# Rates of the recurrence loaded straight into their masked places, tokens issued by GpSimd

## The reference, cut to what matters

```python
delta = xs @ W_delta
Bv = xs @ W_B
Cv = xs @ W_C
deltaA = jnp.exp(jnp.einsum('bld,dn->bldn', delta, A))
deltaB = jnp.einsum('bld,bln->bldn', delta, Bv)
def step(state, inp):
    dA_i, dB_i, x_i, C_i = inp
    state = dA_i * state + dB_i * x_i[:, None, :]
    y = jnp.einsum('bdn,bn->bd', state, C_i)
    return (state, y)
```

## Time and profile before

| what | value |
|---|---|
| median of 3 runs | 7372.27 us (7366.63 to 7378.81) |
| the profiled execution | 7362.99 us, its span 7361.1 us |
| TensorE busy | 6408.9 us (87%) |
| VectorE busy | 6478.1 us (88%) |
| ScalarE busy | 4524.9 us (61%) |
| GpSimd busy | 2747.4 us (37%) |
| the scans (L1059), 2048 long ones | 4468.2 us |
| widening (L1016), 1088 operations | 1619.5 us |
| mean granted TensorE clock | 0.97 of full speed |

### The profile page before, as it was taken

The page is one execution under the profiler, slowest core; times in us unless marked ns, Lnnn a source line. Parts: engine busy times, 40 slices in busy tenths (PEclk is TensorE's granted clock), DMA queues, the critical chain, the costliest instruction groups (busy, mean ns, idle before and its releaser), DMA issues. The chain is left out here.

```text
span 7361.1 us, 173597 instructions
## 1 busy us (share of the span) xinstructions
PE 6408.9 (87%) x52385; PEld 3911.8 (53%) x52385; DVE 6478.1 (88%) x4166; ACT 4524.9 (61%) x9561; POOL 2747.4 (37%) x1996
## 2 busy tenths in 40 slices
PE   8999999999786888888888888888888888888867
PEld 3555547555344555555555555555555555555535
DVE  7888878888557999999999999999999999999962
ACT  7888868888464555555555555555555555555541
POOL 5555445555234333333333333333333333333300
PEclk9999999999898999999999999999999999999985
DMA  6666666666693111111111111111111111111154
GB/s 144 153 156 154 155 144 155 154 154 155 199 321 83 27 27 27 28 27 27 28 26 27 28 27 28 27 27 28 27 26 28 26 29 27 27 27 28 27 171 113
DMA packets 918664, 569.20 MB, mean 77 GB/s; under 512 B 710606, under 2 KB 819054, under 8 KB 917870
## 3 DMA queue, kind: packets, MB, share of 16 engines
q1 hardware_dynamic: 917885, 560.17, 32.1%
HBM read 161.99 MB, written 125.17 MB: 39 GB/s over the span
## 5 line engine op out<-in xcount | busy, mean ns | idle before, releaser
L1059 DVE TENSOR_TENSOR_SCAN states<-decay,enter_ps 128x1024 f32<-128x1024 f32 x2048 | 4468.2, 2262 | 172.3 <-ACT enter_ps L965 167.2
L876 PE MATMUL enter_ps<-s_steps,s_tokens 128*128 128x128 bf16 (+1 forms) x16384 | 2139.3, 311 | 625.6 <-DVE states L1059 514.5
L876 PEld LDWEIGHTS enter_ps<-s_steps,s_tokens 128*128 128x128 bf16 (+1 forms) x16384 | 1596.2, 130 | 1738.5 <-DVE states L1059 1569.4
L950 ACT ACTIVATE decay<-rate_ps 128x504 f32<-128x504 f32 x4096 | 2196.3, 588 | 98.0 <-PE rate_ps L854 23.8
L1016 POOL TENSOR_SCALAR s_wide<-s_rates,mask 128x512 bf16<-128x512 bf16 (+1 forms) x1088 | 1619.5, 1506 | 488.3 <-DMA s_rates<-rates_dram 353.8
L965 ACT COPY enter_ps<-states 128x16 f32<-128x16 f32 x1920 | 363.1, 189 | 1655.4 <-PE enter_ps L876 1649.6
L854 PE MATMUL rate_ps<-s_wide,s_decays 128*128 128x256 bf16 x8192 | 1330.9, 285 | 34.4 <-POOL s_wide L1016 33.7
L243 POOL TENSOR_TENSOR entered<-gates 128x512 f32<-128x512 f32 x512 | 900.9, 1760 | 888.8 <-ACT gates L203 888.8
L900 PE MATMUL y_ps<-states,spread 128*32 128x512 f32 x8320 | 1117.9, 609 | 0.4 <-issue 0.4
L1022 POOL COPY spread<-s_readout 128x64 f32<-128x64 f32 (+1 forms) x272 | 63.6, 234 | 2565.4 <-PE y_ps L900 2009.9
L854 PEld LDWEIGHTS rate_ps<-s_wide,s_decays 128*128 128x128 bf16 x8192 | 897.5, 119 | 95.8 <-issue 36.8
(11 more groups left out here) (154 smaller groups left out, 2310.4 us busy)
## 6 DMA issues: line engine op xcount, KB each, us to landing
rows<-feat SPq DMA_DIRECT2D x1024, 132.0 KB, 2.4
rows<-feat SPq DMA_DIRECT2D x512, 128.0 KB, 2.4
s_steps<-steps_dram SPq DMA_DIRECT2D x4096, 8.0 KB
rows<-feat SPq DMA_DIRECT2D x512, 127.8 KB, 2.4
s_rates<-rates_dram SPq DMA_DIRECT2D x256, 128.0 KB, 2.6
s_tokens<-tokens_dram SPq DMA_DIRECT2D x2048, 16.0 KB
rates_dram<-parts SPq DMA_DIRECT2D x32, 768.0 KB, 4.6
steps_dram<-steps SPq DMA_DIRECT2D x32, 768.0 KB, 8.0
```

Of the source, the lines that this page charges most:

```text
L876: mm = pe.matmul(out.rearrange("p h l -> p l h"), tokens[s][0:n * TERMS, k, :], steps[s][0:n * TERMS, k, 0:n, d:d + half], start=True, sto ...
L950: act.activation(decay[i][:, HEADS // 2 * h:HEADS // 2 * (h + 1), 1:], rate_ps[h][:, :, 0:n], ACT.Exp).then_inc(decay_ready, 1)
L1059: dve.tensor_tensor_scan(out, factor, term, 0.0, ALU.mult, ALU.add).then_inc(scanned, 1)
```

## The change

Channels are put in another order in `rates_dram`: the weights of delta are permuted once (`by_place`, one VectorE copy at the start of the projection), so that the channels with the same i of a group lie next to each other. The decays are loaded in the matching order, 16 small transfers where there were 4. SP then loads the rates in four transfers of 32 partitions each, straight into the places of `wide` that are not zero; the rest of `wide` is zeroed once by VectorE at the start of the recurrence. The tile `rates`, the mask and the four multiplications are gone. The load of rates now waits until the exponents of chunk c-2 are done (`rate_ready`), as the widening did. The 8 transfers of tokens per chunk are issued by GpSimd, with a semaphore of their own that TensorE waits for; GpSimd waits for the entering products of chunk c-2 before them. Steps, readout and y stay with SP.

```diff
--- before.py
+++ after.py
@@ -388,6 +388,7 @@
         sem = Semaphores(nc, ctx, "proj")
         win = sb("win", [128, CHUNKS, 2 * INNER])
         wdelta, wc, wmean = sb("wdelta", [INNER, INNER]), sb("wc", [INNER, INNER]), sb("wmean", [128, 128])
+        by_place = sb("by_place", [INNER, INNER])
         wtok = sb("wtok", [INNER, 3, 128])
         eps = sb("eps", [128, 1])
         x = [sb(f"px{i}", [128, BANK]) for i in range(2)]
@@ -411,7 +412,7 @@
         mean_ps, var_ps, xs_ps, zc_ps, delta_ps = (ps(n) for n in ("mean_ps", "var_ps", "xs_ps", "zc_ps", "delta_ps"))
         tok_ps = [ctx.enter_context(nc.psum_tensor(n, [128, TILES, 128], F32)) for n in ("step_ps", "own_ps", "b_ps")]
 
-        weights_in, eps_set = sem("weights_in"), sem("eps_set")
+        weights_in, eps_set, by_place_set = sem("weights_in"), sem("eps_set"), sem("by_place_set")
         x_in = [sem(f"x_in{i}") for i in range(2)]
         stored = [sem(f"stored{i}") for i in range(2)]
         tok_stored = [sem(f"tok_stored{i}") for i in range(2)]
@@ -484,6 +485,7 @@
         @block.tensor
         def _(pe):
             pe.wait_ge(weights_in, START + WEIGHTS * DMA)
+            pe.wait_ge(by_place_set, START + 1)
 
             def mean(b, i, turn):
                 pe.wait_ge(x_in[i], START + (turn + 1) * CHUNKS * DMA)
@@ -512,7 +514,7 @@
                     n = b * CHUNKS + c
                     pe.wait_ge(xs_ready, START + n + 1)
                     pe.wait_ge(rest1_ready, START + n)
-                    pe.matmul(delta_ps[:, :], wdelta[:, :], xs[i][:, c, :], start=True, stop=True).then_inc(out_ready, 1)
+                    pe.matmul(delta_ps[:, :], by_place[:, :], xs[i][:, c, :], start=True, stop=True).then_inc(out_ready, 1)
                     pe.wait_ge(z_ready, START + (b + 1) * CHUNKS)
                     pe.wait_ge(readout_ready, START + n)
                     pe.matmul(zc_ps[:, :], wc[:, :], xs[i][:, c, :], start=True, stop=True).then_inc(out_ready, 1)
@@ -610,6 +612,10 @@
 
         @block.vector
         def _(dve):
+            dve.wait_ge(weights_in, START + WEIGHTS * DMA)
+            dve.tensor_copy(by_place[:, :].rearrange("p (g i q) -> p g i q", i=QUAD, q=QUARTERS),
+                            wdelta[:, :].rearrange("p (g q i) -> p g i q", i=QUAD, q=QUARTERS)).then_inc(by_place_set, 1)
+
             def centre(b, i, turn):
                 dve.wait_ge(mean_ready, START + b + 1)
                 dve.wait_ge(normed_ready, START + b)
@@ -694,14 +700,12 @@
         readout = [sb(f"s_readout{s}", [STATE, kept[s]]) for s in range(SETS)]
         steps = [sb(f"s_steps{s}", [128, blocks[s], BLOCK, INNER], BF16) for s in range(SETS)]
         tokens = [sb(f"s_tokens{s}", [128, blocks[s], STATE], BF16) for s in range(SETS)]
-        rates = [sb(f"s_rates{s}", [128, GROUPS, kept[s]], BF16) for s in range(SETS)]
         wide = [sb(f"s_wide{s}", [128, GROUPS, QUAD, kept[s]], BF16) for s in range(SETS)]
         decay = [sb(f"decay{i}", [STATE, HEADS, SPAN]) for i in range(RING)]
         decay_end = [sb(f"decay_end{i}", [STATE, HEADS, LAST + 1]) for i in range(RING)]
         y_sb = [sb(f"y_sb{i}", [128, QUAD, INNER]) for i in range(2)]
         none = sb("none", [STATE, HEADS])
         ident = sb("s_ident", [128, 128])
-        mask = sb("mask", [128, QUAD])
         rate_t = sb("rate_t", [STATE, INNER])
         rate = sb("rate", [INNER, STATE])
         rate_left = sb("rate_left", [INNER, STATE])
@@ -713,12 +717,12 @@
 
         consts_in, decays_out, decays_in = sem("consts_in"), sem("decays_out"), sem("decays_in")
         pool_zeroed, vector_zeroed, y_zeroed = sem("pool_zeroed"), sem("vector_zeroed"), sem("y_zeroed")
-        turned, rate_moved, rate1, left1, rate2, rate3, mask_ready = (
-            sem("turned"), sem("rate_moved"), sem("rate1"), sem("left1"), sem("rate2"), sem("rate3"), sem("mask_ready"))
+        turned, rate_moved, rate1, left1, rate2, rate3 = (
+            sem("turned"), sem("rate_moved"), sem("rate1"), sem("left1"), sem("rate2"), sem("rate3"))
         enter_in = [sem(f"enter_in{s}") for s in range(SETS)]
+        tokens_in = [ctx.enter_context(nc.semaphore(f"scan_tokens_in{s}")) for s in range(SETS)]
         rates_in = [sem(f"rates_in{s}") for s in range(SETS)]
         readout_in = [sem(f"readout_in{s}") for s in range(SETS)]
-        widened = [sem(f"widened{s}") for s in range(SETS)]
         spread_ready = [sem(f"spread_ready{s}") for s in range(SETS)]
         rate_ready, decay_ready = sem("rate_ready"), sem("decay_ready")
         enter_ready, carried, scanned = sem("enter_ready"), sem("carried"), sem("scanned")
@@ -727,7 +731,6 @@
         passed = sem("passed")
         block = ctx.enter_context(nc.Block())
 
-        LOADS = BLOCK + TERMS
         HPB = CROWD * GROUPS * 2 + GROUPS
 
         def set_of(c):
@@ -777,24 +780,24 @@
             sp.wait_ge(decays_out, SCAN0 + SPLITS * DMA)
             sp.wait_ge(pool_zeroed, SCAN0 + 1)
             sp.wait_ge(vector_zeroed, SCAN0 + 1)
-            src = decays_dram.rearrange("(g h) e n -> (h e) g n", g=GROUPS)
-            for q in range(QUARTERS):
-                sp.dma_start(decays[32 * q:32 * q + 32, :, q, :], src[32 * q:32 * q + 32, :, :]).then_inc(decays_in, DMA)
+            for i in range(QUAD):
+                for q in range(QUARTERS):
+                    at = 32 * i + TERMS * q
+                    src = decays_dram.rearrange("(g q i) e n -> i q e g n", q=QUARTERS, i=QUAD)[i, q, :, :, :]
+                    sp.dma_start(decays[at:at + TERMS, :, q, :], src).then_inc(decays_in, DMA)
 
             def load(b, c):
                 s, turn, t0 = set_of(c), turn_of(b, c), FULL * c
                 n = SPAN if c < CROWD else LAST
-                sp.wait_ge(widened[s], SCAN0 + turn)
+                sp.wait_ge(rate_ready, halves_to(b, before(c) + 1))
                 sp.sem_inc(passed, 1)
-                src = rates_dram[bass.ds(b, 1), :, :, t0:t0 + n].rearrange("b (g h) e l -> (b h e) g l", g=GROUPS)
-                sp.dma_start(rates[s][:, :, 0:n], src).then_inc(rates_in[s], DMA)
+                for i in range(QUAD):
+                    src = rates_dram[bass.ds(b, 1), :, :, t0:t0 + n].rearrange(
+                        "b (g i q) e l -> i (b q e) g l", g=GROUPS, i=QUAD)[i, :, :, :]
+                    sp.dma_start(wide[s][32 * i:32 * i + 32, :, i, 0:n], src).then_inc(rates_in[s], DMA)
 
                 sp.wait_ge(enter_ready, units_to(b, before(c) + 1))
                 sp.sem_inc(passed, 1)
-                for e in range(TERMS):
-                    a = STATE * (e // SPLITS)
-                    src = tokens_dram[bass.ds(b, 1), t0:t0 + n, a:a + STATE].rearrange("b (k t) n -> (b t) k n", t=BLOCK)
-                    sp.dma_start(tokens[s][e::TERMS, :, :], src).then_inc(enter_in[s], DMA)
                 for t in range(BLOCK):
                     src = steps_dram[bass.ds(b, 1), t0 + t:t0 + n:BLOCK, :].rearrange(
                         "b k (e d) -> e (b k) d", e=TERMS)
@@ -839,14 +842,14 @@
             pe.wait_ge(consts_in, SCAN0 + 2 * DMA)
             pe.wait_ge(y_zeroed, SCAN0 + 1)
             pe.transpose(y_ps[0][:, 0:128], rate_t[:, :], ident[:, :]).then_inc(turned, 1)
-            pe.wait_ge(decays_in, SCAN0 + QUARTERS * DMA)
+            pe.wait_ge(decays_in, SCAN0 + QUAD * QUARTERS * DMA)
             pe.wait_ge(pool_zeroed, SCAN0 + 1)
             pe.wait_ge(vector_zeroed, SCAN0 + 1)
 
             def exponents(b, c, g):
                 s = set_of(c)
                 if g == 0:
-                    pe.wait_ge(widened[s], SCAN0 + turn_of(b, c) + 1)
+                    pe.wait_ge(rates_in[s], SCAN0 + (turn_of(b, c) + 1) * QUAD * DMA)
                 if c < CROWD:
                     for h in range(2):
                         pe.wait_ge(decay_ready, halves_to(b, c) + g * 2 + h - 1)
@@ -865,7 +868,8 @@
             def enters(b, c, g, i):
                 s = set_of(c)
                 if g == 0:
-                    pe.wait_ge(enter_in[s], SCAN0 + (turn_of(b, c) + 1) * LOADS * DMA)
+                    pe.wait_ge(enter_in[s], SCAN0 + (turn_of(b, c) + 1) * BLOCK * DMA)
+                    pe.wait_ge(tokens_in[s], (turn_of(b, c) + 1) * TERMS * DMA)
                 pe.wait_ge(scanned, units_to(b, c) + g - 1)
                 if c < CROWD:
                     for k in range(BLOCKS):
@@ -1004,17 +1008,17 @@
                 z = pool.memset(spread[s][:, :], 0.0)
             z.then_inc(pool_zeroed, 1)
             pool.wait_ge(pool_zeroed, SCAN0 + 1)
-            pool.wait_ge(mask_ready, SCAN0 + 1)
 
             def chunk(b, c):
                 s, turn = set_of(c), turn_of(b, c)
                 n = SPAN if c < CROWD else LAST
-                pool.wait_ge(rates_in[s], SCAN0 + (turn + 1) * DMA)
-                pool.wait_ge(rate_ready, halves_to(b, before(c) + 1))
+                pool.wait_ge(enter_ready, units_to(b, before(c) + 1))
                 pool.sem_inc(passed, 1)
-                for i in range(QUAD):
```

(12 more changed lines are left out.)

## The result

The change ran in 7267.02 us (median of 4 runs, 7264.22 to 7269.51) beside 7375.54 us for the kernel before on the same chip (7366.63 to 7379.01): a ratio of 0.9855, 95% interval 0.9838 to 0.9872. It is faster by 1.4%, inside the forecast's range and 11 us under its point. The profiled execution took 7264.22 us with a span of 7262.5, so 98.6 us less span than before (98.8 us less time; the two medians lie 108.5 us apart).

What follows compares the result with a forecast made beforehand. VectorE's scans bound the kernel, with 147.8 us of idle time to win. Of it 79.3 + 15.7 + 3 = 98 us go and the start adds 4, net -94: 7278 us (profiled execution 7269), range 7262 to 7350.

Steps and rivals of the forecast that it cites:

- Place two: VectorE's wait at the first scan of chunk 3, 14 times, 79.3 us in all; claimed to go entirely.
- the turn of SP's loop: Gap between SP's last y stores and its next transfer, taken as 5.3 us in the chain to chunk 3's steps.
- What follows the first wait: VectorE's waits behind a batch's first wait, 17.2 us over 13 batches; 15.7 us, in five batches, go.
- First waits of the heads: VectorE's wait before a batch's first scan, 47.2 us over 13 batches, laid to ScalarE's loop turn; claimed to remain.
- Small waits: VectorE's remaining waits in the recurrence, 4.1 us in all, of which 3 us go.
- T: Time GpSimd takes to issue one tokens transfer; taken at 1.1 us, ends 0.69 and 2.2.
- The sign of eight transfers in 8 to 10 us: GpSimd's eight tokens transfers of a chunk were to take 8 to 10 us in the new trace.
- both deadlines: Tokens wanted within 17.1 us per plain chunk (T under 1.8), 26.7 at a batch's head (T up to 1.5).
- (a): GpSimd late with tokens at batch heads only, T 1.4: 5 us in 15 batches, time 7353 us; chance 0.17.
- (b): GpSimd issues transfers only between scans, T 2.2, late in chunks and heads: some 7810 us; chance 0.14.
- Rival (c): No effect, SP stays late: rates transfers cost 1.8 us each or its turn grows; 7360 to 7385 us; chance 0.05.
- The start: Start of the recurrence, with more decays and rates transfers and more zeroing: about +4 us, ends +1 and +10.

Runs made afterwards that it cites:

- two: The change with its eight tokens transfers per chunk back on SP: 7643.6 us, ratio 1.0360.
- three: The change with each transfer of rates cut into two, 8 per load, tokens left on GpSimd: 7273.72 us, ratio 0.9870.
- four: The change with each transfer of rates cut into four, 16 per load, tokens left on GpSimd: 7532.3 us, ratio 1.0212.
- eight: The kernel before with only the four y stores after every second chunk moved from SP to GpSimd: 7280.45 us, ratio 0.9887.
- one: The kernel before with only the eight tokens transfers per chunk moved to GpSimd; mask, widening and single rates transfer kept: 7264.62 us, ratio 0.9852.
- ten: The change with two batches written out per turn of TensorE's and ScalarE's loops: 7256.48 us, ratio 0.9838.
- eleven: The change with all 16 batches written out on TensorE and ScalarE, no loop there: 7247.0 us, ratio 0.9820.
- seven: The change with the tokens of a long chunk in 32 transfers on GpSimd, counted on two semaphores: 7736.05 us, ratio 1.0500.

## Why the prediction was right

**Place two, 79.3 us: right.** No wait is left at chunk 3, because SP is early. Experiments two to four and eight show that the waits come and go with how much SP issues, whichever transfers those are: tokens on their own queue did not help with SP full (four), and tokens left on SP did no harm with SP relieved (eight). One term of the sum was too dear without effect: the turn of SP's loop, counted at 5.3 us, took about 3 with the change. It is 4.8 to 5.3 us in every batch of the kernel before and about 3 in experiments one to four and eight; why is open.

**What follows the first wait, 15.7 us: 13.3 measured.** 3.9 us of 17.2 are left; 4029.12 above is one, 1.25 us behind its head. The cause I gave (TensorE's turn exposed by late steps) fits that they fell when the steps came in time. Experiment eight fits it too: of its thirteen heads of this kind, the three with a wait of TensorE for steps just ahead (1.38, 0.21 and 0.37 us) have 4.1, 3.6 and 2.4 us behind the first wait, the other ten at most 1.7. No run tested it apart.

**First waits of the heads, left in place: right** at 47.8 us for 47.2. Their cause was half right, as experiments ten and eleven show: the "issue" of ScalarE was 2.40 us, but taking the turns of ScalarE and TensorE away shortens the head by 1.3 to 1.6 only. The step that failed there is that the whole head was laid to ScalarE's turn; the trace alone doesn't say what is late next.

**Small waits, 3 us: 3.8 measured.** Of the 54.2 us, 47.8 and 3.9 leave 2.5, but 2.23 of these are the first wait of the last batch (at 6635.69), which the kernel before has as a wait for the decays (2.39 at 6730.24). So 4.1 us fell to 0.25.

**T, taken at 1.1 with ends 0.69 and 2.2: mis-sized, at 0.53 outside its own ends.** I chose 1.1 between SP's price for the same transfer and GpSimd's dearest elementwise operation (1.55), with SP's price as the lower end. Neither bounds it; to take SP's price as the floor was the error, since another engine's price is no floor. The sign of eight transfers in 8 to 10 us failed with it: they took 4.24. It cost nothing, because both deadlines had room: 8T + 2.5 is 6.7 us against 17.1, and at the head 16T + 2.2 + 3.2 of turn is 13.9 against 26.7. The turn, between the ends of 0.56 and 5.3, came out at 3.2. The Trainium skill (DMA: Bandwidth & Descriptors, Latency and other measured facts) has the first byte of a transfer from GpSimd come later than of one from SP, and by its ratio T was 1.15 (an estimate). That ratio is of the time to the first byte, and I applied it to the issue: there the runs show the opposite order (0.53 against 0.69). From issue to landing they show no difference to speak of, 2.0 us on the page of the change and 2.1 with the tokens on SP. No run here shows the first byte; for T the measurement decides.

**Rivals (a) and (b): excluded,** T being far under 1.5. For (b) the scans under GpSimd's transfers keep 2.18 us and the transfers 0.53, so neither engine holds the other up. The exemption in the Trainium skill (SBUF — State Buffer, Who interferes with whom) for an operation with at most one SBUF input agrees with that. The mechanism of being late by GpSimd's own sum exists all the same, and experiment seven reached it at a sum of 303 us. **Rival (c): excluded;** the four transfers of rates took 1.84 us (1.6 taken), 0.46 each and not 1.8.

**The start, +4 us: +2.9.** From SP's first transfer of the recurrence (2245.46 us with the change, 2248.26 before) to the first scan it is 31.7 us where it was 28.8. The sixteen transfers of the decays took 0.35 us each, not 0.45:

```profile
2260.74 5.53 SPq L787 DMA_DIRECT2D s_decays<-decays_dram  x16
2266.40 1.79 SPq L797 DMA_DIRECT2D s_wide<-rates_dram  x4
```

**The sum.** Between the first and the last scan the time fell from 4740.9 to 4644.4 us: 96.5 less (forecast 98). Waits for `enter_ps` gave 93.6, the scans' own busy time 5.1, waits for the decays 2.4, and the waits of the short units gave 4.9 back. The tail got 2.2 us shorter, and the projection ended 2.8 us sooner, for which the change shows no cause: so much of the hit is luck. That puts the profiled execution at 7264.2 us where 7269 was forecast. The other 6 us of the 11 are in how a profiled execution stands to its median: I added 9 us, taken from the kernel before; the change's median stands 3 above. The range was a little wider below than its terms: 7278 less 3 for the start and 10 for the heads is 7265, not 7262.

## What to carry to other kernels

Sum what a queue or an issuing engine does over one whole period of the work, its loop's turn included, and compare that with the period of the bounding engine: well under it, moves are free, and over it, nearly each microsecond is paid. Near the edge, look for the one place where the queue is late: the kernel before lost 6.9 us a batch at a sum that just fitted. If it stands there, move the smallest group of transfers that brings it clear, to any engine with room; rearranging data to relieve an engine that had room gains nothing. A cost of the destination that can't be bounded from the trace is best tested against its deadline first, as most sizes may leave the answer the same.

## What the runs showed that was not expected

GpSimd issues a transfer in 0.53 us whether it has 64, 32 or 16 rows (0.64 for steps of 8x4x128), and is cheaper at it than SP (0.69 for the same tokens; 0.46 for the steps). On SP the shape counts: one rates transfer of 128 partitions takes 0.41, a quarter or an eighth or a sixteenth of it still 0.45 to 0.48, so cutting it multiplies the cost. The order of prices is thus not the same on both engines: tokens are the better ones to give to GpSimd.

A turn of a loop whose body fills a batch cost its engine 3.2 us on GpSimd, 2.4 on ScalarE and about 3 on SP, but 4.8 to 5.3 on SP in the kernel before; a turn read from one kernel need not hold for the next. In this kernel, writing out two loops of 14 turns was worth about a fifth of what the change was (23.6 us against 108.5).
